# Attention plus mixture-of-experts block on one core: second batch's query work moved off VectorE, four filler matmuls dropped, router logits turned back by 128-row transpositions

## The reference

```python
# attention, heads H = 8 of width 16, one batch of 128 tokens viewed as (hd=128, lq=256)
x = x + attention(layernorm(x), ctx, ctx, lengths)     # softmax(s_b * q.k), s_b = SCALE * log(length_b)
# feed-forward on layernorm(x), T = 1024 tokens, E = 8 experts, capacity 128 each, hidden 352
probs = softmax(xt @ Wg); eidx = argmax(probs); gate = probs[eidx]
pos = running count of earlier tokens with the same expert; keep = pos < 128
out = gate * keep * (silu(xd @ W1[e]) * (xd @ W3[e])) @ W2[e]      # per expert
shared = silu(xt @ sw1) * (xt @ sw3) @ sw2
x = x + out + shared
```

## Time and profile before

| | us |
|---|---|
| median of three runs (lowest, highest) | 153.0 (152.81, 153.4) |
| the profiled execution's own time | 153.0 |
| its span, first to last instruction | 151.1 |

### The profile page before, as it was taken

One profiled execution on the slowest core, in us unless ns is written; L12 is line 12 of the kernel. 1 busy time (PEld: TensorE's weight loads), 2 busy tenths in 40 slices (PEclk: granted clock), 3 DMA queues, 4 the chain that ended last, 5 costly groups with the idle time before them and its releaser, 6 DMA issues.

```text
span 151.1 us, 3413 instructions
## 1 busy us (share of the span) xinstructions
PE 139.9 (93%) x1254; PEld 95.4 (63%) x1254; DVE 99.3 (66%) x232; ACT 82.1 (54%) x179; POOL 67.9 (45%) x100
## 2 busy tenths in 40 slices
PE   7799999998999999999887999999999999999930
PEld 2365564554554555554443677688999999999720
DVE  0589896778888888887225346877673487774220
ACT  3444275674858676776876357544503676662300
POOL 7116739401850506349992000276600588467250
PEclk9999999999999999999999999999999999999996
DMA  3993454444171700000530099722465622212110
GB/s 70 345 357 118 119 174 143 152 143 146 36 259 39 242 7 5 0 8 0 157 131 4 2 305 323 237 105 70 160 196 156 175 77 80 69 42 91 35 63 35
DMA packets 15825, 18.42 MB, mean 122 GB/s; under 512 B 1981, under 2 KB 15078, under 8 KB 15809
## 3 DMA queue, kind: packets, MB, share of 16 engines
q1 hardware_dynamic: 14368, 14.98, 31.5%
q0 software_dynamic: 1152, 2.97, 6.0%
q10 hardware_dynamic: 288, 0.26, 0.6%
HBM read 14.12 MB, written 4.21 MB: 121 GB/s over the span
## 4 chain that ended last, share of the span: by engine, by line
PE 83%; DVE 4%; DMA 4%; issue 3%; ACT 2%; POOL 1%; SPq 0%; ACTq 0%; POOLq 0%; DVEq 0%
PE bank L1070 20%; PE bank L1110 11%; PE bank L1321 6%; PE bank L1174 6%; PE bank L1175 6%; PE bank L1297 5%; PE bank L1296 5%; PE bank L1262 4%; PE bank L1094 4%; PE bank L1022 3%; PE bank L1124 3%; DMA xs<-in_x 2%; PE bank L1136 2%; PE bank L1079 2%; PE bank L1308 2%
## 5 line engine op out<-in xcount | busy, mean ns | idle before, releaser
L578 DVE TENSOR_REDUCE nm<-bank 128x2 f32<-128x512 f32 x64 | 40.9, 686 | 10.0 <-PE bank L1070 9.5
L843 ACT ACTIVATE pt<-bank 128x512 f32<-128x512 f32 x64 | 35.6, 597 | 17.4 <-PE bank L1094 17.3
L1070 PE MATMUL bank<-kz,qz 32*128 32x256 f32 x256 | 34.6, 400 | 0.9 <-DVE qz L555 0.9
L1094 PE MATMUL bank<-qz,kz 32*128 32x256 f32 x256 | 34.6, 400 | 0.0
L1070 PEld LDWEIGHTS bank<-kz,qz 32*128 32x128 f32 x256 | 21.9, 184 | 13.3 <-DVE nm L578 5.8
L1094 PEld LDWEIGHTS bank<-qz,kz 32*128 32x128 f32 x256 | 21.6, 184 | 1.7 <-ACT pt L843 1.0
L1110 PE MATMUL bank<-pt,vext 128*32 128x256 f32 x256 | 19.8, 390 | 0.1
L502 POOL DMA_INDIRECT expert_rows<-rk,idx_s x8 | 8.7, 1088 | 19.5 <-DVE idx_s L655 17.7
L415 POOL TENSOR_SCALAR qz<-xs,rs,mrs 128x256 f32<-128x256 f32 x14 | 7.7, 561 | 20.0 <-DVE mrs L549 20.0
L517 POOL DMA_INDIRECT xs<-out,rk x8 | 9.9, 1235 | 12.0 <-DMA out<-xs 9.8
L524 POOL DMA_INDIRECT out<-xs,rk x8 | 8.2, 1020 | 8.8 <-DVE xs L741 4.4
(11 more groups left out here) (153 smaller groups left out, 301.1 us busy)
## 6 DMA issues: line engine op xcount, KB each, us to landing
wraw<-in_w SPq DMA_DIRECT2D x10, 352.0 KB, 3.4
wlate<-in_w SPq DMA_DIRECT2D x6, 352.0 KB, 4.4
wraw<-in_w SPq DMA_DIRECT2D x10, 128.0 KB, 3.5
expert_rows<-zero SPq DMA_DIRECT2D x1, 1032.0 KB, 6.7
out<-xs SPq DMA_DIRECT2D x8, 128.0 KB, 2.1
xs<-in_x SPq DMA_DIRECT2D x3, 256.0 KB, 5.1
cs<-in_ctx SPq DMA_DIRECT2D x3, 256.0 KB, 5.3
wlate<-in_w SPq DMA_DIRECT2D x6, 128.0 KB, 4.4
```

What stands on the lines that cost most here:

```text
L578: nc.vector.tensor_reduce(nm[:, b % 2, :, place], scores_bank[:].rearrange("p (u c) -> p u c", u=2), AX_X, ALU.max, negate=True).then_inc( ...
L843: nc.scalar.activation(pt[:, g % NPT, n % 4, :], bank[shifted_bank(n)][:], ACT.Exp).then_inc(exped, 1)
L1070: mm = nc.tensor.matmul(scores_bank[:, u * D:(u + 1) * D], qz[rows, b, half, u * P:(u + 1) * P], kz[rows, b, half, :], start=True, stop=True)
L1094: mm = nc.tensor.matmul(bank[shifted_bank(n)][:, c * D:(c + 1) * D], kz[rows, b, half, c * P:(c + 1) * P], qz[rows, b, half, :], start=Tru ...
```

## The change

Four things. (1) `query_scales(1)` and `eager_queries(1)`, three VectorE instructions between the fourth and the fifth maximum, are gone from VectorE: GpSimd makes batch 1's scale and shift with two small instructions, ScalarE makes half 0 of batch 1's queries. The later `query_scales` get a wait on `q_shift`, so that its count stays in order. (2) The filler matmuls after the first two score groups are two each instead of four. (3) `turn_logits` transposes whole 128 x 128 blocks of `lgt` with the identity, where it multiplied rows 96 to 127 by 8 columns of it; the four results fill bank X, and the logits are read from it at columns 96 to 103 of each block. (4) For that, `lgt` is cleared in all 128 partitions and not in 32.

```diff
-UNREAD = {0: 4, 2: 4, 4: 4, 6: 3, 7: 2, 8: 2, 9: 2}
+UNREAD = {0: 2, 2: 2, 4: 4, 6: 3, 7: 2, 8: 2, 9: 2}
...
-        counts, logits = bank[6], bank[7][:, 0:B * E].rearrange("p (b e) -> p b e", e=E)
+        counts, logits = bank[6], X[:].rearrange("p (b f) -> p b f", b=HALF)[:, :, FL:FL + E]
...   # GpSimd
-            for b in range(EAGER):
-                queries(b, 1)
+            queries(0, 1)
+            pool.wait_ge(q_rstd, 2)
+            pool.wait_ge(len_own, 1)
+            nc.gpsimd.tensor_scalar(rs[:, 1, :], lnown[:, 1, :], rstd[:, 1:2], SCALE, ALU.mult,
+                                    ALU.mult).then_inc(q_rs, 1)
+            pool.wait_ge(q_rs, 2)
+            nc.gpsimd.tensor_scalar(mrs[:, 1, :], rs[:, 1, :], mv[:, 1, 0:1], -1.0, ALU.mult,
+                                    ALU.mult).then_inc(q_shift, 1)
+            queries(1, 1)
...   # VectorE, query_scales(i)
+                if i:
+                    dve.wait_ge(q_shift, i)
...   # VectorE, the loop over turns
-                if t == 1:
-                    query_scales(1)
-                    eager_queries(1)
...
-                    nc.vector.memset(lgt[3 * ROWS:P], 0.0).then_inc(lgt_set, 1)
+                    nc.vector.memset(lgt, 0.0).then_inc(lgt_set, 1)
...   # ScalarE
+            def eager_queries(b):
+
+                act.wait_ge(q_shift, chunk_of[b] + 1)
+                nc.scalar.activation(qz[:, b, 0, :], xs[:, b, :], ACT.Identity, scale=rs[:, b, 0:1],
+                                     bias=mrs[:, b, 0:1]).then_inc(q_eager, 1)
...
             for t in range(STEADY):
+                if t == 1:
+                    eager_queries(1)
...   # TensorE, turn_logits(half)
-                    mm = nc.tensor.matmul(logits[:, HALF * half + b, :], lgt[3 * ROWS:P, b * P:(b + 1) * P],
-                                          cst[3 * ROWS:P, IDENT + 3 * ROWS:IDENT + 3 * ROWS + E], start=True,
-                                          stop=True)
+                    mm = nc.tensor.transpose(X[:, b * P:(b + 1) * P], lgt[:, b * P:(b + 1) * P], ident)
```

More of the change, by code:

```diff
@@ L625, in choose @@
                 dve.wait_ge(lg_turned, part + 1)
-                nc.vector.tensor_reduce(lmax[:, a:z], logits[:, a:z, :], AX_X, ALU.max).then_inc(route, 1)
+                nc.vector.tensor_reduce(lmax[:, a:z], logits, AX_X, ALU.max).then_inc(route, 1)
                 dve.wait_ge(route, routed(part, "lmax"))
-                nc.vector.tensor_tensor(ldif[:, a:z, :], logits[:, a:z, :], lmax[:, a:z].unsqueeze(2).broadcast_to(wide),
+                nc.vector.tensor_tensor(ldif[:, a:z, :], logits, lmax[:, a:z].unsqueeze(2).broadcast_to(wide),
                                         ALU.subtract).then_inc(route, 1)
```

## The result

The changed kernel took 154.56 us against 153.09 for the kernel before beside it: ratio 1.0095, interval 1.0081 to 1.0109. Medians here are of all executions, while the ratios leave out disturbed ones, such as the fourth of this measurement at 157.84 beside three at 154.46 to 154.63. The profiled execution took 154.5, of which 152.6 are span. The same kernel, measured five more times beside the kernel before, gave 151.60, 151.78 and 151.70 on three chips, and 155.63 and 154.57 on two others. So the change has two results, and the profile of the recorded measurement shows where the slower one comes from.

The account below looks back on a forecast made before the run. TensorE was taken to bound the kernel (83% of the chain), with VectorE as tight in the opening and the scatter queue binding at the routing. Opening 0.59 plus routing 0.4 made 0.99: 153.0 - 1.0 = 152.0 us, range 151.4 to 152.8.

Parts of the forecast that it names:

- Opening, -0.59: In the opening, transposed maxima start at 13.00 in place of 13.59, and the 0.59 is carried along.
- VectorE's 0.59: In the opening, three instructions leave VectorE, so the fifth maximum starts at 10.46 instead of 11.05.
- both cuts are needed: In the opening, fewer fillers alone or VectorE's relief alone would bring nearly nothing, as both engines are tight.
- as costed: In the opening, work moved to ScalarE and GpSimd costs nothing, with over 1 us of cover on each.
- Turned logits, 0.39 each: At the routing on TensorE, four transpositions take 0.59 instead of 0.98: 0.39 saved, twice, 0.78 for both halves.
- What of the 0.78 gets through, -0.4: At the routing, the scatter queue's start stays; only fewer collisions shorten it: -0.4, bounds +0.25 and -0.78.
- the 0.82 ahead of the fifth: Before GpSimd's fifth scatter, the 0.82 is its own preparation, not a wait for `idx_s`.
- SP's 0.44: Ahead of the load of the experts' rows, SP waits 0.44 for the eighth scatter's landing.
- everything gets through: Rival, routing: all 0.78 counts beside the opening's 0.59, giving 151.6; needs SP's 0.44 not the last scatter's landing; chance 0.12.
- The collisions with VectorE: At the routing, scatters no longer overlap VectorE's low parts: fifth saves 0.2, eighth 0.4, sixth may gain at most 0.25.
- The clock rival: Rival, opening: with four fewer fillers TensorE's clock falls, +2.5 less the 1.0 gained, giving 154.5; chance 0.07.
- the row transposition has no wait ahead of it: Sign against the forecast, which expects the row transposition near 111.7 after about half a microsecond's wait.

Follow-up runs that it names:

- e1: Kernel before with only the opening's part of the change, logits turned back as before: 152.57 us, ratio 0.9972 to the kernel before (chip 10).
- e4: Changed kernel with the four filler matmuls put back: 152.14 us, ratio 0.9947 to the kernel before (chip 10).
- e6: Changed kernel with VectorE's opening as before, so only fewer fillers and the turned logits: 152.16 us, ratio 0.9934 to the kernel before (chip 4).
- e3: Changed kernel measured again, nothing altered: 151.60 us, ratio 0.9912 to the kernel before (chip 10).
- e12: Kernel before measured against itself, nothing altered: 153.15 us beside 153.12 (chip 15).
- e5: Changed kernel with SP's load of the experts' rows ahead of the fourth store: 151.38 us, ratio 0.9897 to the kernel before (chip 4).
- e13: Kernel before with only the opening's part, measured again: 152.71 us, ratio 0.9974 to the kernel before (chip 15).
- e9: Changed kernel measured again in five rounds, nothing altered: 155.63 us, ratio 1.0096 to the kernel before (chip 12).
- e10: Changed kernel with the experts' rows loaded ahead of the fourth store and fewer fillers: 155.66 us, ratio 1.0106 to the kernel before (chip 12).
- e17: Kernel before with only the turned logits' part, measured again: 155.2 us, ratio 1.0134 to the kernel before (chip 1).
- e2: Kernel before with only the turned logits' part of the change, opening as before: 152.15 us, ratio 0.9942 to the kernel before (chip 10).
- e18: Kernel before with only the opening's part, measured again: 152.76 us, ratio 0.9981 to the kernel before (chip 1).
- e11: Changed kernel with the experts' rows loaded ahead of the fourth store, measured again: 156.57 us, ratio 1.0208 to the kernel before (chip 12).
- e7: Changed kernel with no filler matmuls but the thirteen at the start: 151.47 us, ratio 0.9863 to the kernel before (chip 4).
- e8: Changed kernel measured again, nothing altered: 151.78 us, ratio 0.9918 to the kernel before (chip 4).

## Why the prediction was wrong, step by step

**Opening, -0.59: right in mechanism, a little large.** On VectorE both maxima groups became one, ending at 8.08 + 4.95 = 13.03 for the forecast 12.95; the maxima were turned at 13.08 for 13.00. Before it was 13.59, so 0.51 came here, 0.42 in e1's trace (13.17), and e1 measured 0.48. The term that was too large is VectorE's 0.59: the fifth maximum was to start at 10.46, "if the fifth score matrix is there by then", and that was put at 10.4. In e1's chain the score group ends at 10.64 and the maxima go on at 10.65. That both cuts are needed was right (e4, e6). ScalarE's instruction ended at 10.14 and GpSimd's half of the queries at 9.19, for 10.3 and 9.1: hidden, as costed.

**Turned logits, 0.39 each: too small.** The prediction took 0.59 from the chain as the new price, and said that below it no row goes; the chain of before has four such transpositions at 0.44 as well (13.98, L1045). In TensorE's order each turned logits is worth 0.72, 1.44 for both.

**What of the 0.78 gets through, -0.4: the step that failed on the quiet chips.** What got through was 0.97, 0.24 of the first turned logits and all of the second's 0.72. The prediction saw that VectorE's product holds the first maximum over logits, but not that it holds TensorE's next product too. It held the load of the experts' rows to be released by the eighth scatter and the 0.82 ahead of the fifth to be preparation. Both readings fell. The fifth scatter started 1.02 earlier (102.02 for 103.04) with 0.30 ahead of it, so 0.52 of the 0.82 had been a wait for `idx_s`, and on a quiet chip all scatters had been issued at 107.08 (e3; before: 108.46), 1.38 earlier, of which the opening explains 0.4. And SP's 0.44 does not hang on the scatters. In the twelve traces with the load behind the fourth store and all 128 of the scatters' increments, it follows that store's end by 0.43 or 0.44 each time, but the last increment by anything from 0.29 (e12) to 0.50 (e1); in the trace of before it happened to be 0.44 behind both. So the path was TensorE's fourth product, the add, the store and then the load, and what TensorE had gained by the down products went through it whole. e5 bears it out: with the load ahead of the store it is issued 0.36 earlier. It also shows how near the prediction's reading was, since 0.4 later the scatters would have held. On these chips the time is that of the rival "everything gets through", 151.6 (measured 151.60 to 151.78), and its condition, that SP's 0.44 is not the last scatter's landing, was met. That the number fits so well is partly luck: the opening gave 0.1 to 0.2 less than its 0.59 (e1, e13), and the logits 0.1 to 0.2 more than their 0.78.

**The collisions with VectorE: right in kind, too large in size on the quiet chips, and off the path.** The fifth scatter went from 1.19 to 0.97. The eighth went from 1.37 to 0.97 only where a late release had held the low part back, as in the recorded measurement; in e3 it is 1.15, since it starts at 105.93 inside a low part that ends at 106.23. e1, where low parts and scatters moved together, keeps 1.19 and 1.37. The Trainium skill, "SBUF — State Buffer", "SBUF: two separate sides", says that VectorE's hold of the port pair delays the descriptors; these rows agree, for each lengthened scatter ends 0.85 or 0.86 behind VectorE's low part (107.08 and 106.23 in e3, 108.46 and 107.61 before). Nothing waits for them.

**The sign: a step that was not there.** On the recorded measurement's chip the releases of the first two down products come 2.3 and 2.7 late. The prediction let the down products' adds follow TensorE at once, as they do in the traces of before, and had no rival for a release that arrives after the work; 2.1 of the 2.9 are lost there, so all of the turned logits' gain and 1.2 more. Why they come late is open. The clock rival (154.5) matches the number and not the mechanism: in the recorded measurement the clock from 7 to 140 is full. It does fall in e9, e10 and e17, but between 107 and 113, behind the stall, and not in the opening. The thirteen first fillers did run longer there (to 6.74, before to 6.01), but the first scores waited for their queries and started at 6.85 (before 6.92).

Of the marks that the prediction set for itself, "the row transposition has no wait ahead of it" did not come true: about 0.1 was left of the forecast half microsecond (in e3 the last matmul ahead ends at 111.18, the transposition starts at 111.32). It stood at 111.3 on the quiet chips, not at 111.7.

## What to carry to other kernels

A gap behind a DMA issue is not a wait for the semaphore that the code names until the releaser's time is set beside it: in the trace of before, the last scatter's landing and the fourth store's end both stood at 110.16, and only several traces side by side, and one run with the two exchanged, told them apart. The price of an instruction in the chain or in the timeline is not what its absence gives; what counts is how much nearer its neighbours on both sides come, and whether the next of them then waits for another engine (here 0.72 each, of which one kept 0.24). A gain of half a per cent to one per cent that shifts two engines against each other has to be measured on more than one chip: here the same 151.6 us kernel took 154.6 to 155.6 in three other measurements, and of the four versions that were tried under both conditions (the changed kernel, e5, e2 and e1) only e1, the opening alone, was slower in none (0.9972, 0.9974, 0.9981). And when two engines are both tight, neither cut shows without the other (e4, e6).

## What the runs showed of the hardware

- Releases by TensorE arrived 2.2 to 2.8 us behind the modelled end of the matmul in the recorded measurement and on chips 12 and 1, in each of the six profiled executions that had the new logits, at the first two down products; on chips 4, 10 and 15 the same program has none over 0.15. The traces of the late ones, and e18's, hold 2323 to 2359 semaphore updates, the others 2595 to 2600.
- After TensorE had stood 1.7 us at such a place, the granted clock fell in some executions (0.58 from 110 to 113 in e9) and not in others (1.00 there in e11): 36 matmuls took 6.08 and 4.56.
- The load behind the fourth store follows that store's end by 0.43 to 0.44, while the scatters' last increment lies 0.29 to 0.50 ahead of it; in e11, where it stands behind a third store that itself followed another at once, by 0.04. What the 0.44 consists of is open.
- Without any filler after the start the clock stayed full in the profiled execution of e7 (148.7 span), but its four executions lie between 150.54 and 153.31 where those of e2, e3, e4 and e8 spread by 0.25 to 0.4. The mean granted clock was 0.996 in the profiled one and 0.970 in the longest.
- Four float32 transpositions of 128 x 128 took TensorE 0.72 less, from neighbour to neighbour, than four products of 32 x 128 by 32 x 8, recorded as eight matmuls (0.58 for 1.30, e3 and e1).
- A scatter issued by GpSimd inside one of VectorE's low parts ended 0.85 or 0.86 behind that part, 1.12 to 1.37 long instead of 0.97 (before, e1, e2, e3).
